# GNN layer on one core: W_uh h made for every node group in the first part, edge sums in four banks of their own

## The chip, the cores and the metric

The kernel runs on one core of one Trainium2 chip. The metric is the time of one execution on the device, in microseconds. A core has TensorE (PE, with its weight loads as PEld), VectorE (DVE), ScalarE (ACT), GpSimd (POOL) and SyncE (SP), which issues the plain DMAs.

## The reference

```python
h = relu(layernorm(x))                                   # 50000 nodes x 128
msg = relu(relu([h[src], h[dst], edge_attr] @ Wm1 + bm1) @ Wm2 + bm2)   # 25000 edges, sorted by dst
agg = segment_sum(msg, dst, 50000)
u = relu([h, agg] @ Wu1 + bu1)                           # = relu(h @ W_uh + agg @ W_ua + bu1)
out = x + h + (u @ Wu2 + bu2)
```

All of it is float32. dst is drawn as 50000 * u**2, so the first nodes receive many edges and the later ones few.

## The kernel before

There are two parts, each with one program per engine.

The first part has 49 steps of 512 edges and 1024 nodes (two groups of 512 nodes). GpSimd gathers the rows of x at both ends of the 512 edges with eight indirect DMAs a step (L278). DVE and ACT normalise edge ends and nodes, TensorE transposes four tiles of 512 columns (L509) and ACT writes them with a relu into `ht` (L457): 0 and 1 are the ends of the edges, 2 and 3 the two node groups. TensorE makes the messages in three pieces (L519 to L521, L529, L535), and ACT moves each from PSUM. Messages stay in SBUF, already multiplied by W_ua. For the even group of a step TensorE also makes W_uh h (L526), which ACT copies over `ht[2]` (L462). The node tiles of both groups (for the odd group still h itself) go to the scratch `ht_scratch`, and x + h to `xh_scratch`.

The second part visits 98 groups of 512 nodes. For each edge tile of 128 edges that can reach the group, DVE makes a one-hot matrix (`hot`, L693), ACT the high part and GpSimd the low part of the messages (`high` L733, `low` L659), and TensorE adds low x hot and high x hot into the group's bank (L784, L785). Which tiles they are is read from a table: at the start of every group each of the four engines loads the group's two numbers into two registers (L626). Every group has at least two tiles, the first group more than twenty. `hot`, `high` and `low` have slots for two groups, and a group may be prepared when the group two before it has been summed (L706, L745). Two banks hold edge sums, two hold outputs.

- For an even group the sum is copied by ACT (`pre_u`, L764), GpSimd adds W_uh h (L680), and ACT makes u (L751). For an odd group TensorE first puts W_uh h into the bank (L810), adds the edge tiles, and ACT makes u straight from the bank.
- The bias of the output is a matmul (`row_sel`, L822) for an even group; for an odd one GpSimd adds it to x + h (L683).
- TensorE multiplies u by W_out (L825), DVE adds x + h (L717), SP stores. SP loads the two scratch tiles of a group ahead, in four slots each.

The engines' programs are unrolled by 4 (TensorE, GpSimd), 8 (DVE) and 2 (ACT, by pairs of groups).

Of the kernel before, what the change touches and what calls it, by code (L numbers as in the profile page):

```python
# [52 lines left out]
def build(nc, x, ends, dst_rows, dst_cols, edge_t, wm1, bm1, wm2, bm2, wu1, bu1, wu2, bu2, out):  # L71
    with ExitStack() as ctx:
# [10 lines left out]
        ht_d = nc.dram_tensor("ht_scratch", (GROUPS, P, W), F32).ap()  # L83
# [15 lines left out]
        ht_i, xh_i = sb("ht_i", [P, 4, W]), sb("xh_i", [P, 4, W])  # L99
# [26 lines left out]
        s_ldh = [sem(f"ht_loaded{i}") for i in range(4)]  # L126
# [7 lines left out]
        s_sum, s_pre_u = sem("edge_sums_copied"), sem("pre_u_ready")  # L134
        s_ut = sem("u_ready")
        s_xb = sem("xh_biased")
# [6 lines left out]
        def load_h(sp, g, slot):  # L143
            sp.dma_start(ht_i[:, slot, :], ht_d[g]).then_inc(s_ldh[slot], 16)
# [5 lines left out]
        with ExitStack() as one:  # L150
# [38 lines left out]
            def sync_1(sp):  # L189
# [40 lines left out]
                def body(s, slot, use):  # L230
                    if not below(s, STEPS - 1) and below(s, STEPS + 1):

                        for g in range(2 * (s - STEPS + 1), 2 * (s - STEPS + 2)):
                            load_h(sp, g, g)
                            load_xh(sp, g, g)
# [4 lines left out]
                    if at_least(s, 3):  # L240
                        to, half = bass.ds(2 * (s - 3), 2), (slot + 1) % 2
                        sp.wait_ge(s_ht, 4 * (s - 2))
                        sp.wait_ge(s_hu, s - 2)
                        sp.dma_start(ht_d[to].rearrange("g p f -> p g f"), ht[:, half, 2:4]).then_inc(s_sto[half], 16)
# [194 lines left out]
            def scalar_1(act):  # L439
                act.wait_ge(s_w, 16 * 11)  # L440

                def body(s, slot, use):
# [45 lines left out]
                    if has_norm:  # L488
# [3 lines left out]
                        relu(range(2, 4))  # L492

                run_steps(act, STEPS + 2, 4, STEPS - 1, 4, body)

            def tensor_1(pe):
# [14 lines left out]

                def messages(s, slot, use, part):
                    if part == 0:
# [9 lines left out]
                        pe.wait_ge(s_ht, 4 * s + 3)  # L523
                        if at_least(s, 1):
                            pe.wait_ge(s_hu, s)
                        pe.matmul(p_hu[:], w_uh[:], ht[:, slot % 2, 2, :], start=True, stop=True).then_inc(s_hus, 1)  # L526
# [30 lines left out]
        with ExitStack() as two:  # L557

            hot = sb("hot", [P, 10, W], F32R, on=two)
            high, low = sb("high", [P, 10, D], F32R, on=two), sb("low", [P, 10, D], F32R, on=two)  # L560
# [5 lines left out]
            out_o = sb("out_o", [P, 4, W], on=two)  # L566
            p_agg, p_out = banks[0:2], banks[2:4]

            def sync_2(sp):
# [28 lines left out]
            class EdgeTiles:  # L598

                def __init__(self, eng, name):
                    self.eng = eng
                    self.regs = [eng.alloc_register(f"{name}_range{i}") for i in range(2)]
# [18 lines left out]
                def visit(self, g, par, regular, more):  # L623

                    eng = self.eng
                    eng.load(self.regs, ranges[0:1, bass.ds(g * 2, 2)])  # L626
                    lo = eng.snap(self.regs[0], min_val=0, max_val=ET - 2)
                    hi = eng.snap(self.regs[1], min_val=2, max_val=ET)
                    regular(lo, 2 * par, 0)
                    with eng.If(hi > lo + 2):  # L630
                        more(lo + 2, 4 + par, None)
                        with eng.If(hi > lo + 3):
                            with eng.Fori(lo + 3, hi, 4) as k:
                                more(k, 6, 0)
                                more(k + 1, 7, 0)
                                with eng.If(hi > k + 2):
                                    more(k + 2, 8, 1)
                                    more(k + 3, 9, 1)
                    regular(lo + 1, 2 * par + 1, 1)

            def gpsimd_2(pool):
# [15 lines left out]
                def low_parts(g, slot):  # L657
# [11 lines left out]
                    tiles.visit(g, slot % 2, regular, more)  # L669

                def body(g, slot, use):
                    if below(g, GROUPS):
                        low_parts(g, slot)
                    if not at_least(g, 1):
                        bias_low()
                    prev = (slot - 1) % 4
# [10 lines left out]
            def vector_2(dve):  # L687
                tiles = EdgeTiles(dve, "dve")

                def onehots(g, slot):  # L690
# [14 lines left out]
                    if at_least(g, 2):  # L705
                        dve.wait_ge(s_agg, g - 1)  # L706
                    tiles.visit(g, slot % 2, regular, more)
# [166 lines left out]
```

## Time and profile before

| | us |
|---|---|
| median of 3 runs | 1107.69 |
| lowest and highest | 1104.02, 1116.73 |
| span of the profiled execution, first to last instruction | 861.7 |
| first part, to the last copy of messages | about 534 |
| second part, first full pair of groups to the end | 565.5 to 861.7 |

The profile gives its own execution by its span alone, and no time of that execution was kept beside it. The median holds 246.0 us more than the span; what lies outside the span is not in any row. One digit of the page's slices is a tenth of a slice of 21.5 us. A busy PE is not PE at its peak: its records overlap.

### The profile page before, as it was taken

Reading aid. Unit: us, or ns where it says so; the run is one execution under the profiler, and the core shown is the slowest. Engines: PE = TensorE matmul, PEld = TensorE weight load, DVE = VectorE, ACT = ScalarE, POOL = GpSimd, SP = SyncE. Lnnn points to the kernel's source line nnn. Section 1 sums busy time; section 2 is a strip of 40 time slices with the busy share of each in tenths; the row PEclk is TensorE's granted clock in tenths of the full one; section 3 lists DMA queues with packets and bytes.
Section 4 is the critical chain, followed back from the end, with each engine's and each line's share of the span. In section 5 each row is a group of like instructions: output and inputs, shape, how many; then the busy total and the mean of one; then the engine's idle time right before and its main releaser. Section 6 shows DMA issues by size and latency. Waiting matters only on the chain. (4 is left out here: it accounts for less than half of the span.)

```text
span 861.7 us, 19736 instructions
## 1 busy us (share of the span) xinstructions
PE 727.2 (84%) x3207; PEld 446.1 (52%) x3208; DVE 666.2 (77%) x2285; ACT 533.4 (62%) x1238; POOL 696.4 (81%) x834
## 2 busy tenths in 40 slices
PE   0688878888898888887787787899999999999998
PEld 0344444444444444443454343566677777676666
DVE  3877787777777777777787775899999988776775
ACT  0666776767676667666687665545555665555554
POOL 7777777777777777777777750899999999898996
PEclk9998998989899999899899999999999999999999
DMA  6466666666666666666676674036688888899897
GB/s 161 125 205 209 219 222 203 215 212 211 203 208 201 204 202 203 206 212 206 209 243 218 196 233 156 0 114 186 191 241 256 273 285 273 275 288 286 285 290 237
DMA packets 99721, 184.50 MB, mean 214 GB/s; under 512 B 15101, under 2 KB 16512, under 8 KB 99700
## 3 DMA queue, kind: packets, MB, share of 16 engines
q1 hardware_dynamic: 87156, 158.57, 56.4%
q0 software_dynamic: 12544, 25.72, 11.0%
q14 instruction: 16, 0.13, 0.1%
q8 instruction: 5, 0.08, 0.0%
HBM read 107.25 MB, written 76.98 MB: 214 GB/s over the span
## 5 line engine op out<-in xcount | busy, mean ns | idle before, releaser
L278 POOL DMA_INDIRECT xg<-x_in,ends_now x392 | 383.3, 978 | 116.2 <-issue 112.9
L693 DVE TENSOR_SCALAR hot<-node,dst_f,minus_base 128x512 fp32r<-128x512 f32 x303 | 212.3, 753 | 42.9 <-issue 30.6
L659 POOL TENSOR_TENSOR low<-msgs,high 128x128 fp32r<-128x128 f32 x303 | 175.4, 603 | 40.7 <-ACT high L733 39.0
L450 ACT ACTIVATE zn<-xn,shift,rstd 128x128 f32<-128x128 f32 x343 | 141.9, 482 | 46.8 <-DVE shift L384 46.1
L784 PE MATMUL bank<-hot,low 128*128 128x512 f32 x303 | 149.1, 492 | 14.3 <-POOL low L659 7.1
L341 DVE BATCH_NORM_STATS2 bn<-xg 128x6 f32<-128x128 f32 x392 | 80.4, 277 | 103.2 <-DMA xg<-x_in,ends_now 103.2
L733 ACT ACTIVATE high<-msgs 128x128 fp32r x303 | 90.1, 310 | 81.3 <-issue 47.2
L785 PE MATMUL bank<-hot,high 128*128 128x512 f32 x303 | 120.4, 397 | 0.0
L509 PE MATMUL bank<-ident,xg 128*128 128x128 f32 x392 | 70.4, 314 | 57.1 <-DVE xg L403 56.7
L526 PE MATMUL bank<-ht,w_uh 128*128 128x512 f32 x98 | 62.8, 727 | 54.0 <-ACT ht L462 54.0
L509 PEld LDWEIGHTS bank<-ident,xg 128*128 128x128 f32 x392 | 49.1, 158 | 112.8 <-issue 87.5
L825 PEld LDWEIGHTS bank<-w_out,u_t 128*128 128x128 f32 x784 | 101.8, 191 | 10.2 <-issue 2.5
L403 DVE TENSOR_SCALAR xg<-xg,mean,rstd 128x128 f32<-128x128 f32 x392 | 106.3, 362 | 0.0
L457 ACT ACTIVATE ht<-bank 128x512 f32<-128x512 f32 x196 | 104.9, 588 | 0.7 <-PE bank L509 0.7
L825 PE MATMUL bank<-w_out,u_t 128*128 128x128 f32 x784 | 103.9, 276 | 0.0
L336 DVE BATCH_NORM_STATS2 bn<-xn 128x6 f32<-128x128 f32 x392 | 98.4, 277 | 0.0
L784 PEld LDWEIGHTS bank<-hot,low 128*128 128x128 f32 x303 | 57.4, 190 | 74.2 <-issue 50.8
L717 DVE TENSOR_TENSOR out_o<-bank,xh_i 128x512 f32<-128x512 f32 x98 | 67.0, 684 | 16.8 <-PE bank L825 15.7
L390 DVE SCALAR_TENSOR_TENSOR xh_o<-zn,xn 128x512 f32<-128x512 f32 x98 | 67.3, 687 | 3.7 <-issue 2.0
L683 POOL TENSOR_TENSOR xh_i<-xh_i,b_out 128x512 f32<-128x512 f32 x49 | 66.7, 1361 | 0.5 <-DMA xh_i<-xh_scratch 0.5
L680 POOL TENSOR_TENSOR pre_u<-pre_u,ht_i 128x512 f32<-128x512 f32 x49 | 64.4, 1314 | 1.4 <-ACT pre_u L764 1.3
L785 PEld LDWEIGHTS bank<-hot,high 128*128 128x128 f32 x303 | 57.9, 191 | 13.1 <-issue 9.2
(85 smaller groups left out, 968.6 us busy)
## 6 DMA issues: line engine op xcount, KB each, us to landing
ht_scratch<-ht SPq DMA_DIRECT2D x49, 512.0 KB
xh_scratch<-xh_o SPq DMA_DIRECT2D x49, 512.0 KB
ht_i<-ht_scratch SPq DMA_DIRECT2D x98, 256.0 KB, 3.7
xh_i<-xh_scratch SPq DMA_DIRECT2D x98, 256.0 KB, 3.5
out<-out_o SPq DMA_DIRECT2D x97, 256.0 KB, 3.6
xn<-x_in SPq DMA_DIRECT2D x48, 512.0 KB
xg<-x_in,ends_now POOLq DMA_INDIRECT x392
edge<-edge_t_in SPq DMA_DIRECT2D x49, 64.0 KB
```

Of the source, the lines that this page charges most:

```text
L278: pool.indirect_dma_start(xg[:, slot, t, :], None, x, bass.IndirectOffsetOnAxis(ap=ends_now[:, slot8, t:t + 1], axis=0)).then_inc(s_xg[slo ...
L336: dve.bn_stats(bn[:, slot % 2, 8 + t, :], xn[:, slot, t, :])
L403: ins = dve.tensor_scalar(to, of, mean[:, slot % 2, t:t + 1], rstd[:, slot % 2, t:t + 1], ALU.subtract, ALU.mult)
L450: ins = act.activation(zn[:, prev % 2, t - 8, :], xn[:, prev, t - 8, :], ACT.Identity, bias=shift[:, prev % 2, t:t + 1], scale=rstd[:, pre ...
L457: act.activation(ht[:, prev % 2, q, :], p_tr[q][:], ACT.Relu).then_inc(s_ht, 1)
L509: ins = pe.transpose(p_tr[q][:, j * P:(j + 1) * P], of, ident[:])
L659: return pool.tensor_tensor(low[:, at, :], msgs[:, k, :], high[:, at, :].bitcast(F32), ALU.subtract)
L693: return dve.tensor_scalar(hot[:, at, :], node[:], dst_f[:, bass.ds(k, 1)], minus_base[:, bass.ds(g, 1)], ALU.subtract, ALU.is_equal)
L733: return act.activation(high[:, at, :], msgs[:, k, :], ACT.Copy)
L784: pe.matmul(to, low[:, at, :], hot[:, at, :], start=start, stop=False, skip_group_check=True)
L785: return pe.matmul(to, high[:, at, :], hot[:, at, :], start=False, stop=stop, skip_group_check=True)
L825: ins = pe.matmul(p_out[half][:, j * D:(j + 1) * D], u_t[:, half, j * P:(j + 1) * P], w_out[:], start=not even, stop=True, skip_group_chec ...
```

## The change

W_uh h is made for both groups of a step in the first part: a second matmul of 512 columns and a second ACT move, now with the bias b_u1 in it (Identity with bias in place of Copy). The scratch holds W_uh h + b_u1 for all groups. In the second part the matmul L810 is gone. An even group goes as before (ACT copy, GpSimd add, ACT relu); for an odd group DVE adds the loaded tile to the bank and ACT makes the relu from SBUF. The output bias is a matmul for every group, and GpSimd's add of it (L683) is gone. Edge sums and outputs have four banks each, `hot`, `high` and `low` have slots for four groups, the registers of four groups are loaded at once (eight numbers), and DVE's last step lies one group later. The output tile lies where `xh_o` was.

```diff
-                    def w_h(s, half):
-                        act.wait_ge(s_hus, s + 1)
-                        act.activation(ht[:, half, 2, :], p_hu[:], ACT.Copy).then_inc(s_hu, 1)
+                    def w_h(s, half, n):
+                        act.wait_ge(s_hus, 2 * s + n + 1)
+                        act.activation(ht[:, half, 2 + n, :], p_hu[:], ACT.Identity, bias=b_u1[:]).then_inc(s_hu, 1)
...
                     if at_least(s, 3):
-                        w_h(s - 3, (slot - 3) % 2)
+                        w_h(s - 3, (slot - 3) % 2, 1)
                     if has_msg:
                         act.wait_ge(s_m1, s - 1)
                         act.activation(m1t[:], p_m1[:], ACT.Relu, bias=b_m1[:]).then_inc(s_m1t, 1)
-                        if not below(s, STEPS + 1):
-                            w_h(s - 2, slot % 2)
+                        w_h(s - 2, slot % 2, 0)
...
+                def w_h(s, slot, n):
+                    pe.wait_ge(s_ht, 4 * s + 3 + n)
+                    if n or at_least(s, 1):
+                        pe.wait_ge(s_hu, 2 * s + n)
+                    pe.matmul(p_hu[:], w_uh[:], ht[:, slot % 2, 2 + n, :], start=True, stop=True).then_inc(s_hus, 1)
...
                     if part == 1:
                         pe.wait_ge(s_m1t, s + 1)
                         pe.matmul(p_m2[:], w_msg[:], m1t[:], start=True, stop=True).then_inc(s_m2, 1)
+                        w_h(s, slot, 1)
...
-            p_agg, p_out = banks[0:2], banks[2:4]
+            out_o = xh_o[:].rearrange("p a b w -> p (a b) w")
+            p_agg, p_out = banks[0:4], banks[4:8]
...
-                        if slot % 2 == 1:
-                            sp.wait_ge(s_pre_u, 2 * use + slot // 2)
-                        else:
-                            sp.wait_ge(s_agg, g - 2)
-                        load_h(sp, g + 1, (slot + 1) % 4)
+                        sp.wait_ge(s_ut, g - 2)
+                        load_hu(sp, g + 1, (slot + 1) % 4)
...
-                def visit(self, g, par, regular, more):
+                def visit(self, g, slot, regular, more):
-                    eng.load(self.regs, ranges[0:1, bass.ds(g * 2, 2)])
+                    if slot == 0:
+                        n = 8 if below(g, GROUPS - 3) else 2 * (GROUPS - g)
+                        eng.load(self.regs[0:n], ranges[0:1, bass.ds(g * 2, n)])
...
-                    if slot % 2 == 1:
-                        pool.wait_ge(s_sum, 2 * use + slot // 2 + 1)
-                        pool.wait_ge(s_ldh[prev], 16 * use + 16)
-                        pool.tensor_tensor(pre_u[:], pre_u[:], ht_i[:, prev, :], ALU.add).then_inc(s_pre_u, 1)
-                    elif at_least(g, 2):
-                        pool.wait_ge(s_ldx[prev], 16 * (use - (slot < 1)) + 16)
-                        pool.tensor_tensor(xh_i[:, prev, :], xh_i[:, prev, :], b_out[:], ALU.add).then_inc(s_xb, 1)
+                    if slot % 2 == 0 and at_least(g, 2):
+                        pool.wait_ge(s_sum, 2 * use + slot // 2)
+                        pool.wait_ge(s_ldh[(slot - 2) % 4], 16 * (use - (slot < 2)) + 16)
+                        pool.tensor_tensor(pre_u[:], pre_u[:], hu_i[:, (slot - 2) % 4, :], ALU.add).then_inc(s_pre_e, 1)
...
+                def add_w_h(g, slot, use):
+                    dve.wait_ge(s_agg, g + 1)
+                    dve.wait_ge(s_ldh[slot], 16 * use + 16)
+                    dve.tensor_tensor(hu_i[:, slot, :], p_agg[slot][:], hu_i[:, slot, :], ALU.add).then_inc(s_pre_o, 1)
...
                 def body(g, slot, use):
                     if below(g, GROUPS):
                         onehots(g, slot)
-                    if at_least(g, 3):
-                        finish(g - 3, (slot - 3) % 4, use - (slot < 3), 2 * use + slot // 2 - 2)
+                    if slot % 2 == 1 and at_least(g, 2) and below(g, GROUPS + 2):
+                        add_w_h(g - 2, (slot - 2) % 4, use - (slot < 2))
+                    if at_least(g, 4):
+                        finish(g - 4, slot, use - 1)
...
+                    if slot % 2 == 1 and at_least(g, 3):
+                        act.wait_ge(s_pre_e, 2 * use + slot // 2)
+                        u_of(g - 3, (slot - 3) % 4, pre_u[:])
+                        act.wait_ge(s_pre_o, 2 * use + slot // 2)
+                        u_of(g - 2, (slot - 2) % 4, hu_i[:, (slot - 2) % 4, :])
...
-                        pe.wait_ge(s_ldh[slot], 16 * use + 16)
-                        if at_least(g, 2):
-                            pe.wait_ge(s_ut, g - 1)
-                        pe.matmul(to, w_uh[:], ht_i[:, slot, :], start=True, stop=False, skip_group_check=True)
+                    if at_least(g, 4):
+                        pe.wait_ge(s_pre_o if slot % 2 else s_sum, 2 * use + slot // 2 - 1)
```

In ACT and DVE the wait ahead of a group's tiles becomes `s_agg >= g - 3` from the fifth group on (before: `s_agg >= g - 1` from the third), and TensorE's program is unrolled by 8, ACT's by 4.

## Rows read from the trace of the kernel before

**Rows 1.** The page: each engine's busy time, share of the span, instructions.

```profile
PE 727.2 (84%) x3207; PEld 446.1 (52%) x3208; DVE 666.2 (77%) x2285; ACT 533.4 (62%) x1238; POOL 696.4 (81%) x834
```

**Rows 2.** Three stretches: length; busy PE, PEld, DVE, ACT, POOL; clock, DMA share, GB/s.

```profile
40.00:500.00 460.00, 379.69 (x1511) 201.13 (x1510) 351.23 (x1687) 316.61 (x713) 354.38 (x378) 0.93 0.64 208
565.50:719.10 153.60, 151.73 (x759) 110.64 (x758) 145.20 (x205) 88.52 (x225) 153.45 (x207) 1.00 0.74 226
719.10:852.40 133.30, 125.96 (x662) 92.81 (x661) 97.45 (x151) 76.89 (x175) 119.01 (x151) 1.00 0.90 286
```

**Rows 3.** Waits in 40 to 500: total us, times, longest.

```profile
POOL xg L278 <- issue: 102.8, 347, 0.3
DVE bn L341 <- DMA xg<-x_in,ends_now: 97.1, 33, 4.8
PE bank L526 <- ACT ht L462: 50.7, 27, 3.4
PE bank L509 <- DVE xg L403: 25.6, 47, 1.2
...
POOL xg L278 <- PE bank L509: 3.0, 10, 0.3
```

**Rows 4.** Groups in 40 to 500: count, busy us, mean ns, idle before.

```profile
L278 POOL DMA_INDIRECT xg<-x_in,ends_now  x357 | 348.1, 975 | 105.9 <-issue 102.8 <-PE bank L509 3.0
L526 PE MATMUL bank<-ht,w_uh 128*128 128x512 f32 x90 | 58.3, 735 | 50.7 <-ACT ht L462 50.7
L462 ACT ACTIVATE ht<-bank 128x512 f32<-128x512 f32 x45 | 26.5, 589 | 0.0
```

**Rows 5.** Groups in 565.5 to 719.1 (23 pairs of groups).

```profile
L693 DVE TENSOR_SCALAR hot<-node,dst_f,minus_base 128x512 fp32r<-128x512 f32 x159 | 119.8, 808 | 7.9 <-issue 6.6 <-PE bank L785 0.7
L659 POOL TENSOR_TENSOR low<-msgs,high 128x128 fp32r<-128x128 f32 x160 | 94.6, 618 | 0.1
L683 POOL TENSOR_TENSOR xh_i<-xh_i,b_out 128x512 f32<-128x512 f32 x24 | 32.9, 1369 | 0.0
L717 DVE TENSOR_TENSOR out_o<-bank,xh_i 128x512 f32<-128x512 f32 x46 | 31.3, 680 | 0.5
```

**Rows 6.** Timeline of GpSimd, one pair of groups with six tiles: start, us.

```profile
641.99 1.84 POOL L659 TENSOR_TENSOR low<-msgs,high 128x128 fp32r<-128x128 f32 x3
...
648.08 1.83 POOL L659 TENSOR_TENSOR low<-msgs,high 128x128 fp32r<-128x128 f32 x3
```

**Rows 7.** Timeline of DVE, a late group.

```profile
800.31 1.18 DVE L693 TENSOR_SCALAR hot<-node,dst_f,minus_base 128x512 fp32r<-128x512 f32 x2 [0.66 <-issue]
```

**Rows 8.** The chain of waits within one pair of 12 tiles: start, us, what.

```profile
565.69 0.23 PE bank L822
565.92 0.89 PE bank L825 x8
566.81 0.86 PE bank L810 x2
567.67 0.23 PE bank L784
...
570.96 1.00 POOLq L626
```

**Rows 9.** Register loads in 533 to 561 and from 600: ns, least/median/most.

```profile
L626 POOLq TENSOR_LOAD <-ranges x3: 518/528/888, 534.7 to 558.3; - x3
...
L626 DVEq TENSOR_LOAD <-ranges x86: 523/600/1460, 604.4 to 851.1; - x86
```

**Rows 10.** Groups in 719.1 to 852.4 (24 pairs of groups).

```profile
L693 DVE TENSOR_SCALAR hot<-node,dst_f,minus_base 128x512 fp32r<-128x512 f32 x103 | 67.2, 695 | 22.3 <-issue 15.1 <-PE bank L785 7.1
```

**Rows 11.** Two stretches with much DMA, columns as in Rows 2.

```profile
765.00:770.00 5.00, 4.42 (x22) 2.66 (x20) 3.23 (x6) 2.69 (x6) 4.51 (x6) 1.00 0.99 350
...
820.00:840.00 20.00, 18.74 (x100) 13.46 (x99) 15.62 (x23) 11.08 (x25) 17.95 (x25) 1.00 0.92 294
```

**Rows 12.** DMA issues: KB each, median us to landing; 98 loads of xh_i likewise.

```profile
ht_i<-ht_scratch SPq DMA_DIRECT2D x98, 256.0 KB, 3.7
```

More of the change, by code:

```diff
@@ L124, in build @@
         s_sto = [sem(f"scratch_stored{i}") for i in range(2)]
-        s_ldh = [sem(f"ht_loaded{i}") for i in range(4)]
+        s_ldh = [sem(f"hu_loaded{i}") for i in range(4)]
         s_ldx = [sem(f"xh_loaded{i}") for i in range(4)]
@@ L140, in build, with load_hu @@
         s_out = [sem(f"out_stored{i}") for i in range(4)]
[L143 to L144 removed]
+        def load_hu(sp, g, slot):
+            sp.dma_start(hu_i[:, slot, :], hu_d[g]).then_inc(s_ldh[slot], 16)
         def load_xh(sp, g, slot):
@@ L492, in body @@
                         relu(range(2, 4))
+                    if not below(s, STEPS + 1):
+                        w_h(s - 2, slot % 2, 1)
                 run_steps(act, STEPS + 2, 4, STEPS - 1, 4, body)
@@ L521, in messages @@
                         pe.matmul(p_m1[:], w_edge[:], edge[:, slot, :], start=False, stop=True).then_inc(s_m1, 1)
[L523 to L526, printed above, removed]
+                        w_h(s, slot, 0)
                     if part == 1:
@@ L557, in build @@
         with ExitStack() as two:
-            hot = sb("hot", [P, 10, W], F32R, on=two)
-            high, low = sb("high", [P, 10, D], F32R, on=two), sb("low", [P, 10, D], F32R, on=two)
+            hot = sb("hot", [P, 16, W], F32R, on=two)
+            high, low = sb("high", [P, 16, D], F32R, on=two), sb("low", [P, 16, D], F32R, on=two)
             pre_u = sb("pre_u", [P, W], on=two)
@@ L603, in __init__ @@
                     self.eng = eng
-                    self.regs = [eng.alloc_register(f"{name}_range{i}") for i in range(2)]
+                    self.regs = [eng.alloc_register(f"{name}_range{i}") for i in range(8)]
                     self.count = eng.alloc_register(f"{name}_count")
@@ L703, in more, with finish @@
                         onehot(k, at).then_inc(s_hot_x, 1)
-                    if at_least(g, 2):
-                        dve.wait_ge(s_agg, g - 1)
-                    tiles.visit(g, slot % 2, regular, more)
-                def finish(g, slot, use, odd_before):
+                    if at_least(g, 4):
+                        dve.wait_ge(s_agg, g - 3)
+                    tiles.visit(g, slot, regular, more)
+                def add_w_h(g, slot, use):
+                    dve.wait_ge(s_agg, g + 1)
+                    dve.wait_ge(s_ldh[slot], 16 * use + 16)
+                    dve.tensor_tensor(hu_i[:, slot, :], p_agg[slot][:], hu_i[:, slot, :], ALU.add).then_inc(s_pre_o, 1)
+                def finish(g, slot, use):
                     dve.wait_ge(s_o, g + 1)
-                    if slot % 2 == 1:
-                        dve.wait_ge(s_xb, odd_before + 1)
-                    else:
-                        dve.wait_ge(s_ldx[slot], 16 * use + 16)
+                    dve.wait_ge(s_ldx[slot], 16 * use + 16)
                     if at_least(g, 4):
                         dve.wait_ge(s_out[slot], 16 * use)
-                    dve.tensor_tensor(out_o[:, slot, :], p_out[slot % 2][:], xh_i[:, slot, :], ALU.add
-                                      ).then_inc(s_fin, 1)
+                    elif not at_least(g, 1):
+                        for half in range(2):
+                            dve.wait_ge(s_sto[half], 32 * ((STEPS + 1 - half) // 2))
+                    dve.tensor_tensor(out_o[:, slot, :], p_out[slot][:], xh_i[:, slot, :], ALU.add).then_inc(s_fin, 1)
                 def body(g, slot, use):
@@ L742, in more, with u_of @@
                         part(k, at).then_inc(s_hi_x, 1)
-                    if at_least(g, 2):
-                        act.wait_ge(s_agg, g - 1)
-                    tiles.visit(g, slot % 2, regular, more)
-                def u_of(g, half, of):
+                    if at_least(g, 4):
+                        act.wait_ge(s_agg, g - 3)
+                    tiles.visit(g, slot, regular, more)
+                def u_of(g, slot, of):
                     if at_least(g, 2):
                         act.wait_ge(s_o, g - 1)
-                    act.activation(u_t[:, half, :], of, ACT.Relu, bias=b_u1[:]).then_inc(s_ut, 1)
+                    act.activation(u_t[:, slot % 2, :], of, ACT.Relu).then_inc(s_ut, 1)
                 def body(g, slot, use):
@@ L779, in sums @@
                 def sums(g, slot, use):
-                    to = p_agg[slot % 2][:]
-                    even = slot % 2 == 0
+                    to = p_agg[slot][:]
                     def add(at, stop, start=False):
@@ L790, in regular @@
                         pe.wait_ge(s_lo, 2 * g + n + 1)
-                        ins = add(at, n == 1, n == 0 and even)
+                        ins = add(at, n == 1, n == 0)
                         if n == 1:
```

92 lines of the change are left out of this document (38 added, 54 removed).

## The prediction

> **What bounds the kernel now.** I read the page first for its totals [rows 1], then split the span by stages, because a mean over two parts with different limits hides both [rows 2]. The first part advances by one step of eight gathers each 460 / (357 / 8) = 10.31 us. Its bound is in the groups [rows 4]: a gather takes 975 ns and leaves 296 ns of issue time behind it (105.9 / 357), 1.27 us together, and eight are 10.2 us. GpSimd waits for another engine for 3.0 us in all of this stretch, while DVE waits 97.1 us for gathered rows [rows 3]. TensorE is busy 379.7 of 460 us, 8.51 us a step, and idle 1.80 us a step. So the first part goes at the pace at which GpSimd issues gathers, with TensorE second.
>
> In the second part I take a pair of groups as the unit, since the two kinds of groups alternate. From 565.5 to 719.1 there are 23 pairs of 6.68 us with 159 tiles (6.9 a pair), and GpSimd is busy 153.45 of 153.6 us with DVE behind it at 145.2 [rows 2]. The timeline shows what that full GpSimd does in a pair of six tiles: 6.09 us from 641.99 to 648.08, of which six low parts at 0.60 us (three in 1.84, overlapping a little) are 3.6 us and the two long adds (L680, L683) 1.25 us each [rows 6]. From 719.1 to 852.4 there are 24 pairs of 5.55 us with 4.3 tiles each. No engine is full there (TensorE 126.0, GpSimd 119.0, DVE 97.5 of 133.3 us), DMA has a share of 0.90 at 286 GB/s, and DVE waits 15.1 us before its one-hots for nothing but its own sequencer [rows 2, 10]. That is the register load: 523 to 1460 ns each group [rows 9], and in the chain it stands between two pieces of work, 1.00 us of it at 570.96 [rows 8].
>
> **First part, step by step.** Each of the 49 steps gets one more 512-column matmul on TensorE and one more 589 ns move on ACT [rows 4]. The present matmul costs 58.3 us over 45 steps, 1.30 us; at full clock two such passes take 0.86 us start to start, as L810 shows [rows 8]. That makes TensorE 8.51 + 1.30 = 9.81 us of 10.31 a step. I cost it at nothing on the path: its cover is the idle 1.80 us, of which 50.7 us (1.13 a step) lie before L526, where TensorE waits for ACT, and 25.6 us (0.57) before the transposes L509, where it waits for DVE [rows 3]. The new matmul stands just before those transposes and eats that wait first. If the cover were gone the whole 1.30 us would show, less the 0.50 left: see the rivals. TensorE's new wait (for the first move by ACT, before the second matmul) has the transposes and message matmuls queued behind it; but the message matmul L529, of the same size, stands in front, and ACT's move takes 0.59 us. ACT is busy 316.6 of 460 us, so 26.5 us more fits. The store of the scratch waits for the same move of ACT as before, and its bytes and number are unchanged. When the gathers are over this part drains, and there the last move of ACT comes after the last copy of messages: +0.6 us on the path, with a semaphore 0.7. **First part: +0.7 us**, bounds 0 and +1.5 apart from the rival.
>
> In the stretch of the first part the granted clock is 0.93, a mix of 2.4 GHz and 1.2 GHz; in the second part, where TensorE is hardly ever idle, it is 1.00 throughout [rows 2]. In "TensorE: Matmul & The Clock Gate", Part 1, the Trainium skill says that TensorE falls to half rate after idling. By that rule the extra matmul would raise the clock of the first part; the sum takes no credit for it.
>
> **Second part, early pairs.** Taken off GpSimd: L683, 1369 ns, once a pair [rows 5]. GpSimd's load falls from 6.67 us a pair by 1.25 start to start, to about 5.4. Taken off TensorE: L810, 0.86 us a pair; added there: one L822, 0.23 [rows 8]. So neither sets the pace any more, and what is late next is DVE. Its load is 145.2 / 23 = 6.31 us a pair. The change adds one PSUM add of the shape of L717, 680 ns [rows 5]. It also relieves DVE: a one-hot takes 808 ns on average here [rows 5], against 0.59 us in a late group (two in 1.18) [rows 7]. The excess, 0.218 x 159 = 34.7 us, I put to waiting beside the 47 long adds of GpSimd (24 of L683 and 23 of L680) (0.74 us each), as the one-hots that run beside those are the long ones; the low parts cost only hundreds of nanoseconds. One of two long adds goes: -0.74 a pair if that is so, nothing if the one-hots are slowed by GpSimd's work in general. DVE's load becomes 6.31 + 0.68 - 0.74 = 6.25, or 6.99 without relief. To 6.25 I add 0.1 for what remains of its idle time (8.4 us in 23 pairs now, most of it before register loads). That is 6.35 against 6.68: **-0.33 a pair, -7.6 us in 23 pairs**; bounds -0.74 x 23 = -17 (all of DVE's idle time gone and more) and (6.99 - 6.68) x 23 = +7.
>
> Waits that change: a group is prepared when the group four before it is summed, not two. The chain now passes from the sums of one group through the preparation of the next [rows 8]; with four slots this loop opens, and TensorE follows the producers. DVE's new add waits for the sums of the group two before, and behind it are queued the output add and the next one-hots; TensorE has two groups of time for these, so I cost it at nothing. ACT's relu of the odd group now waits for DVE's add, with the next high parts behind it and GpSimd's low parts behind those; GpSimd has 1.2 us a pair to spare for that. SP's order stays load, load, store, each behind waits of about the same age.
>
> **Late pairs.** By the same steps a pair needs on DVE 97.45 / 24 + 0.69 less half of 0.105 x 103 / 24, that is 4.5 us; on GpSimd 119.0 / 24 - 1.37 = 3.6; on TensorE 4.3 tiles x 0.46 + 2 x 0.89 + 2 x 0.23 = 4.2 [rows 2, 5, 8, 10]. The transfers are what is left: a pair moves six tiles of 256 KB [rows 12], 1.573 MB, and now takes 5.55 us for them. The fastest 20 us that I found run at 294 GB/s with a share of 0.92, a stretch of 5 us at 350 with 0.99 [rows 11]. Those would be 5.35 and 4.5 us a pair. I take 5.2 us (302 GB/s), nearer to the long stretch, since a rate must be held for 130 us: **-0.35 a pair, -8.4 us in 24 pairs**; bounds -0.2 and -0.95 a pair (DVE's 4.5 plus 0.1). The stretch ahead of 565.5, with the first two groups, I cost at nothing: more than half of its tiles belong to one group and go through the slots that are as few as before. The drain at the end gains an add by DVE of 0.7 us, and loses a register load of as much.
>
> **The register load.** Four loads of two registers become one of eight. The trace has no load of eight. From below it costs as much as one of two (0.52 us), from above four times that, 2.1 us, in one piece. I take about 1 us, near the end below: at 534.7 all four engines load together, eight registers in all, and the slowest took 888 ns [rows 9]. Then it is nearly covered by the operation queued on the engine.
>
> "Runtime: NRT & Kernel Launch", in the section on instruction fetch, the Trainium skill gives about 200 ns for each register, even in bulk. By that figure eight would be an estimated 1.6 us, which speaks for the upper end and for the second rival.
>
> **Sum.** 0.7 - 7.6 - 8.4 = -15.3 us. The profiled execution goes from a span of 861.7 to 846.4; with the 246.0 us that the median holds outside the span, 1107.7 becomes **1092 us** (1088 to 1099).
>
> **Rivals.**
> - *The transfers don't bind late* (350 GB/s can be held): late pairs go at 4.6 us, 24 x 0.95 = -22.8, with the early gain and the first part -29.7, 1078 us. For it: single stretches of 5 us at that rate. Against: never for 20 us.
> - *The load grows with its registers*: 2.1 us in one piece, of which 0.6 is covered by one queued operation, so 1.5 us a four-group round, 0.75 a pair, on DVE. Early pairs become 6.25 + 0.75 = 7.0, +7.4 us in all; late ones 4.5 + 0.75 = 5.25, -7.2. With +0.7 that is 1109 us. Loads of up to 1460 ns speak for it.
> - *DVE takes GpSimd's place without relief*: early +7, late -8.4, first part +0.7: 1107 us.
> - *TensorE becomes the bound of the first part* (slower): the waits for DVE and ACT are tied to the step and aren't eaten. Then a step is 8.51 + 1.30 + 1.80 = 11.6 us in place of 10.31, +1.3 x 48 = +62, less 16: 1154 us. It decides as soon as load and waits exceed 10.31, that is when less than 1.30 of the 1.80 us of idle time can be used; if 0.5 us of step time showed it would be 1116. Against it: the new matmul stands where TensorE waits, and GpSimd waited for TensorE hardly at all, so that a late step can be caught up.
>
> **Chances.** The forecast 0.45, transfers not binding 0.13, load by registers 0.20, no relief 0.12, TensorE in the first part 0.10. A difference of 1% (11 us) is about what a measurement of this kernel can tell from none. Faster by more (under 1096.6): most of the first and all of the second, 0.56; slower by more (over 1118.8): 0.08; the rest 0.36. The range leaves out half of the fast rival and the slow one: 1078 to 1112.
>
> **What the profile after should show.** Steps of the first part still of 10.3 us, L526 twice as often, and the idle time before it smaller. GpSimd no longer full in early pairs and DVE at 97% or more; one-hots shorter than 808 ns. A pair of six tiles in about 5.75 us. Late, DMA at or over 300 GB/s with a share above 0.95 and register loads only each fourth group. I am wrong if the step of the first part grows beyond 10.5 us, if the loads take 2 us and stand in the chain, or if a late pair stays at 5.5 us with DMA still at 286 GB/s: then latency along the chain of a group, not transfers, set its pace.

## The result, and the profile after

The kernel after takes 1114.1 us (median of 20 runs, 1108.7 to 1120.6), the kernel before 1109.5 (20 runs, 1098.5 to 1116.7): ratio 1.007, 95% interval 1.0045 to 1.0096. The forecast was 1092, a gain of 15.3 us; what came is a loss of 4.6. Medians here are of all runs of a kernel, while ratios leave out slow runs (over 1.5% above the fastest of their kernel), so in a few places the two don't divide out exactly.

The profiled execution of after took 1113.5 us with a span of 1110.7: only 2.8 us lie outside its span. So the 246 us that the median of before holds above its span of 861.7 can't be time outside the span. The traced execution of before can't have been like the timed ones. Its chip is not known, but the experiments met both cases: on three chips the first part of every run went without stalls (e1 to e6, e15 to e18), on two it stalled in every kernel that gathers without a pause (e7 to e14). Each chip was used at one time only, so whether it is the chip or its condition at that time is not known; below I say chips with and without stalls. The first part of after ends at 804.5 us (before: 534.4), the second takes 306.2 us (before: 327.3). First the three stretches that answer to [rows 2]: length, busy time of PE, PEld, DVE, ACT, POOL, then clock, DMA share, GB/s.

```profile
70.00:690.00 620.00, 406.56 (x1420) 203.99 (x1419) 314.43 (x1493) 310.26 (x670) 302.76 (x331) 0.78 0.43 136
837.50:983.20 145.70, 132.27 (x736) 107.28 (x734) 144.69 (x231) 77.12 (x226) 120.31 (x184) 1.00 0.78 240
983.20:1101.10 117.90, 106.30 (x638) 88.41 (x636) 113.58 (x173) 64.67 (x175) 87.91 (x128) 1.00 0.97 319
```

In the first line every engine is idle for a third of the time or more, GpSimd for half, and the clock is 0.78. In the second, DVE has taken GpSimd's place (99% busy against 83%). In the third DMA is at a share of 0.97. The waits of the first part of after, answering to [rows 3]:

```profile
POOL ends_now L258 <- PE bank L492: 232.5, 20, 14.8
DVE r L351 <- ACT sd L448: 196.6, 33, 13.7
ACT msgs L467 <- remote: 127.9, 18, 11.4
```

GpSimd, which waited 3.0 us for the transposes in before, now waits 232.5 us for them, 11.6 us in each of 20 waits. One round of the timeline of after (start, us, idle time before and what ended it; "remote" is a semaphore whose sender the profile doesn't name):

```profile
394.18 0.19 POOL L258 COPY ends_now<-ends_all 128x16 int32 x1 [12.24 <-PE bank L492]
...
401.97 1.06 PE L522 MATMUL bank<-w_ua,m2t 128*128 128x128 f32 x8
...
403.25 0.58 ACT L439 ACTIVATE ht<-bank 128x512 f32<-128x512 f32 x1
...
405.54 0.18 DVE L343 SCALAR_TENSOR_TENSOR var<-pair,sq 128x16 f32<-128x16 f32 x1 [1.70 <-remote]
...
406.93 0.60 ACT L439 ACTIVATE ht<-bank 128x512 f32<-128x512 f32 x1 [3.09 <-remote]
...
413.70 0.95 POOL L260 DMA_INDIRECT xg<-x_in,ends_now  x1 [0.30 <-issue]
417.60 0.60 ACT L467 ACTIVATE msgs<-bank 128x512 f32 x1 [10.07 <-remote]
...
425.94 0.21 POOL L258 COPY ends_now<-ends_all 128x16 int32 x1 [11.30 <-PE bank L492]
```

GpSimd issues gathers from 394.9 to 414.7 without a pause. For the first 9 us the others work at their usual pace. Then handovers come late: DVE waits 1.7 us at 405.54 for a semaphore that its own instruction before last was to raise, and ACT stands idle for 10 us until 417.60, though the matmuls that it waits for (L522) ended at 403.0. In most rounds of this trace that copy starts 2.7 to 3.0 us after the last gather has been issued. Only then does the work go on, at its usual pace again, and GpSimd stands still until the transposes of 425.6. A round of two steps takes 31.9 us on average, where two steps took 20.7 in the trace of before.

The second part, one-hots and low parts of the 23 early pairs of after, to be read against [rows 5], and its register loads against [rows 9]:

```profile
L672 DVE TENSOR_SCALAR hot<-node,dst_f,minus_base 128x512 fp32r<-128x512 f32 x161 | 107.1, 720 | 0.7 <-PE bank L771 0.3 <-issue 0.3
L645 POOL TENSOR_TENSOR low<-msgs,high 128x128 fp32r<-128x128 f32 x160 | 88.4, 579 | 25.4 <-ACT high L720 25.4
```

```profile
L612 DVEq TENSOR_LOAD <-ranges x23: 352/1148/1591, 857.6 to 1095.9; - x23
L612 POOLq TENSOR_LOAD <-ranges x23: 548/597/1430, 857.6 to 1095.2; - x23
```

### The profile page after: what moved, and what is told of

Same layout as the page of the kernel before. It is cut to its first block and busy times, and to the rows that moved or that the text cites. A ratio compares the mean times of both kernels' runs of the same rounds, so it can differ in the third digit from the quotient of the medians.

```text
span 1110.7 us, 19375 instructions
## 1 busy us (share of the span) xinstructions
PE 779.5 (70%) x3256; PEld 472.2 (43%) x3257; DVE 686.8 (62%) x2334; ACT 547.6 (49%) x1287; POOL 620.9 (56%) x785
## 5 line engine op out<-in xcount | busy, mean ns | idle before, releaser
L499 PE MATMUL bank<-ht,w_uh 128*128 128x512 f32 x196 | 132.4, 763 | 111.1 <-ACT ht L444 108.6
L351 DVE RECIPROCAL r<-sd 128x16 f32<-128x16 f32 x49 | 12.4, 253 | 253.2 <-ACT sd L448 238.9
L508 PE MATMUL bank<-ht,w_src 128*128 128x512 f32 x98 | 69.3, 796 | 137.0 <-issue 75.5
L770 PE MATMUL bank<-hot,low 128*128 128x512 f32 x303 | 132.0, 435 | 5.0 <-POOL low L645 4.7
L499 PEld LDWEIGHTS bank<-ht,w_uh 128*128 128x128 f32 x196 | 37.5, 227 | 200.4 <-ACT ht L439 126.2
L385 DVE TENSOR_SCALAR xg<-xg,mean,rstd 128x128 f32<-128x128 f32 x392 | 105.7, 355 | 2.0 <-issue 2.0
L467 ACT ACTIVATE msgs<-bank 128x512 f32 (+1 forms) x49 | 29.2, 596 | 143.4 <-remote 139.0
L720 ACT ACTIVATE high<-msgs 128x128 fp32r x303 | 80.6, 304 | 38.5 <-PE bank L771 18.9
L444 ACT ACTIVATE ht<-bank,b_u 128x512 f32<-128x512 f32 x98 | 68.1, 695 | 46.3 <-PE bank L499 37.4
L492 PE MATMUL bank<-ident,xg 128*128 128x128 f32 x392 | 54.7, 284 | 40.8 <-DVE xg L385 32.1
L508 PEld LDWEIGHTS bank<-ht,w_src 128*128 128x128 f32 x98 | 17.9, 229 | 145.8 <-issue 85.4
```

The lines of the kernel that those rows point to most:

```text
L385: ins = dve.tensor_scalar(to, of, mean[:, slot % 2, t:t + 1], rstd[:, slot % 2, t:t + 1], ALU.subtract, ALU.mult)
L499: pe.matmul(p_hu[:], w_uh[:], ht[:, slot % 2, 2 + n, :], start=True, stop=True).then_inc(s_hus, 1)
L720: return act.activation(high[:, at, :], msgs[:, k, :], ACT.Copy)
L770: pe.matmul(to, low[:, at, :], hot[:, at, :], start=start, stop=False, skip_group_check=True)
```

## The experiments

Every ratio is to runs of before on the same chip. **Chips without stalls** (before 861): one for e1 to e3, one for e4 to e6, one for e15 to e18. **Chips with stalls** (before 1130 and 1111): one for e7 to e10, one for e11 to e14.

**e1, before unchanged.**

> The kernel before, unchanged, profiled again. Theory A (the timed runs of both kernels stall in the first part, and the profiled execution of before was one without the stalls): span near 1105 us, a first part of some 775 us in place of 534 with stalls of GpSimd of about 11 us in every second step, and a second part of 327 us as in the trace of before. Theory B (before has no stalls, and 246 us lie outside its span while only 3 us lie outside that of after): span near 862 us again, time near 1109.

862.5 us, span 860.7, first part 533.0 us, no stall; before beside it 861.4. Theory B's span of 862 came, but not its time of 1109: here only 1.7 us lie outside the span, so the 246 us are no fixed cost. It needed a trace of before on a chip with stalls (e11).

**e2, only the first part's share.** To the kernel before:

```diff
-                        act.activation(ht[:, half, 2, :], p_hu[:], ACT.Copy).then_inc(s_hu, 1)
+                        act.activation(ht[:, half, 2 + n, :], p_hu[:], ACT.Copy).then_inc(s_hu, 1)
...
                         pe.matmul(p_m2[:], w_msg[:], m1t[:], start=True, stop=True).then_inc(s_m2, 1)
+                        w_h(s, slot, 1)
```

> The kernel before with only the first part's share of the change: the second W_uh matmul and ACT move of each step; the second part is unchanged and applies W_uh once more to the odd groups, so their output is not that of the reference. Theory A (the stall ends at a fixed point of a chain through TensorE and ACT, so added work there is paid in every round of two steps): 49 matmuls of 0.86 to 1.3 us, 20 to 35 us slower than before, 1130 to 1145. Theory B (hidden beside the gathers, my prediction): within 2 us of before.

865.6 us, ratio 1.0033 (1.0009 to 1.0057). Without stalls the extra work is hidden: the last step of gathers starts at 501.7 us against 501.5 in e1. The 4 us come behind the gathers: the last copy of messages ends at 535.4 against 533.0, the first one-hot starts at 539.6 against 534.4.

**e3, only the second part's share.** To the kernel after, the matmul and move are as before:

```diff
-                        w_h(s, slot, 1)
...
-                        act.activation(ht[:, half, 2 + n, :], p_hu[:], ACT.Identity, bias=b_u1[:]).then_inc(s_hu, 1)
+                        act.activation(ht[:, half, 2, :], p_hu[:], ACT.Copy).then_inc(s_hu, 1)
```

> The kernel after without the second W_uh matmul and ACT move in the first part: the odd groups add h in place of W_uh h, and the bias b_u1 is left out, so the output is not that of the reference. Theory A: the second part's gain alone, 20 us (306 against 327 us), so 1085 to 1092. Theory B (the second part gives nothing, and something else in the first part moved): 1105 to 1115. If the stalls of the first part react to the extra work, the difference to the kernel after is 20 to 30 us.

842.1 us, ratio 0.979 (0.9756 to 0.9826): the gain of the second part alone.

**e4, after unchanged.**

> The kernel after, unchanged. Theory A (the time depends on whether this chip lets the first part stall; the second part gains 20 us on any chip, and the first part loses 3 to 4 us without stalls, some 25 us with them): where the kernel before takes about 861 us, the kernel after takes 845 (ratio 0.981); where before takes about 1109, it takes 1114. Theory B (the whole difference of 1.007 is in the kernels, not in the stalls): ratio 1.00 to 1.01 on any chip.

847.0 us, ratio 0.982 (0.9788 to 0.9855). The same kernel that lost 0.7% gains 1.8% here. The ratios of e2 and e3 multiplied are 0.982 as well. e15, on a third such chip, gave 0.980.

**e5, register loads for each group.** To the kernel after:

```diff
-                    if slot == 0:
-                        n = 8 if below(g, GROUPS - 3) else 2 * (GROUPS - g)
-                        eng.load(self.regs[0:n], ranges[0:1, bass.ds(g * 2, n)])
+                    eng.load(self.regs[2 * slot:2 * slot + 2], ranges[0:1, bass.ds(g * 2, 2)])
```

> The kernel after with the register loads of before: two registers, once a group, into each group's own pair of registers. Theory A (a load of eight costs nearly the same as one of two, so one load in four groups saves idle time of DVE, which sets the pace): 5 to 12 us slower than the kernel after, as each group's load leaves 0.2 to 0.6 us of idle time on DVE. Theory B (a load of eight takes four times as long and stands in the path): same or faster than the kernel after.

848.4 us beside 847.0, ratios 0.9844 (0.9814 to 0.9875) and 0.9822. The two can't be told apart by time; the profiled spans differ by 3.5 us. Theory A's 5 to 12 us did not come, and nothing speaks for Theory B: the load is worth a few us at most.

**e6, GpSimd's second long add put back.** To the kernel after:

```diff
+                    if slot % 2 == 1 and at_least(g, 2):
+                        if at_least(g, 4):
+                            pool.wait_ge(s_twice, 2 * use + slot // 2 - 1)
+                        pool.tensor_tensor(b_out[:], node[:], b_out[:], ALU.add).then_inc(s_twice, 1)
```

> The kernel after with GpSimd's second long add a pair put back: it adds node and b_out in SBUF for each odd group, 128 x 512, and nobody waits for it. Theory A (DVE's one-hots are held up beside each long add by 0.74 us): 47 x 0.3 to 0.74 us, 14 to 35 us slower than the kernel after, and the mean one-hot of the early pairs back near 800 ns. Theory B (the long adds don't hold DVE up; GpSimd has the time to spare): within 3 us of the kernel after.

865.0 us, 18 us more than e4, ratio 1.004 (1.0019 to 1.0058): the gain of the second part is gone. Nobody waits for this add. The one-hots of the early pairs of e4, then of e6:

```profile
L672 DVE TENSOR_SCALAR hot<-node,dst_f,minus_base 128x512 fp32r<-128x512 f32 x161 | 108.0, 726 | 1.0 <-issue 0.6 <-PE bank L771 0.3
```

```profile
L677 DVE TENSOR_SCALAR hot<-node,dst_f,minus_base 128x512 fp32r<-128x512 f32 x161 | 120.6, 804 | 0.6 <-issue 0.6
```

At 804 ns they are back at the 808 of before [rows 5]. An early pair takes 6.89 us against 6.40, a late one 5.21 against 4.93. DVE is busy 157.9 of 158.5 us in e6's early pairs, so the longer one-hots go straight into the time; GpSimd is not full (151.9). The trace shows where they are longer: of the 160 one-hots there, the 60 that run beside a long add for more than 0.2 us average 1044 ns, the other 100 average 653. In the trace of before it is 1058 ns for 55 and 667 for 103.

**e7, the second matmul behind the first transposes.** To the kernel after:

```diff
-                        w_h(s, slot, 1)
                     if part == 2:
+                        w_h(s, slot, 1)
```

> The kernel after with the second W_uh matmul of a step moved from in front of the first two transposes to behind them. Where the first part has no stalls both orders are hidden beside the gathers: Theory A 842 to 848 us, as the kernel after (847) within 3 us. Theory B (the place of the matmul costs even beside running gathers): 3 us or more faster than the kernel after. Where it has stalls: Theory A 20 to 25 us faster than the kernel after (1090), since the matmul no longer stands between DVE's normalised ends and the transposes for which GpSimd waits; Theory B no different from it.

This chip stalls: 1135.1 us, before 1129.7, ratio 1.0014 (0.9975 to 1.0053). Theory A's 20 us did not come. The kernel after did not run on this chip, so whether the moved matmul is a few us better stays open (after's ratios on two other chips are 1.007 and 1.010).

**e8 to e10, stop and go by a tighter wait.** In before, after and moved:

```diff
-                        pool.wait_ge(s_tr, 4 * (s - 2) - 2)
+                        pool.wait_ge(s_tr, 4 * s - 2)
```

> The kernel before with GpSimd's wait tightened, so that a pair of gather steps starts only when the first two transposes of the step just gathered are made. It copies, on a chip without stalls, the stop and go that the trace of the kernel after shows: two steps of gathers, 20.4 us, then a wait of some 10 to 12 us. Both theories: 1080 to 1160 us. It is the base for the next two.

> The kernel after with the same tightened wait. Theory A (in each wait the second W_uh matmul stands in front of the transposes, 0.9 to 1.1 us on the path in each of 24 waits): first part 21 to 27 us longer than in the locked kernel before, second part 16 to 20 us shorter, so 0 to +10 us, ratio to it 1.000 to 1.009, as the 1.007 of the result. Theory B (the extra work is hidden in stop and go too): 13 to 19 us faster than the locked kernel before.

> The kernel with the moved matmul and the same tightened wait. Theory A: 18 to 25 us faster than the locked kernel after, 13 us or more faster than the locked kernel before. Theory B (it is ACT's extra move, not the place of the matmul, that costs): within 5 us of the locked kernel after.

They came to the chip with stalls, not to one without, so the wait came on top of the late handovers: 1213.3, 1232.3 and 1233.0 us, ratios 1.074 (1.070 to 1.078), 1.090 (1.084 to 1.096) and 1.092 (1.088 to 1.096). The split, from the traces (first part; then means over 21 rounds: GpSimd's wait, of it up to ACT's last square root, and from there to GpSimd's restart):

| | first part | wait | to the root | from it |
|---|---|---|---|---|
| e8, before | 889.4 | 16.21 | 10.03 | 6.19 |
| e9, after | 924.9 | 17.55 | 10.39 | 7.16 |
| e10, moved | 920.1 | 17.49 | 11.33 | 6.16 |

e9 is 19 us slower than e8, where its Theory A said 0 to 10: its first part is 35.5 us longer, more than the 21 to 27 forecast. The moved matmul leaves the stretch after the root (7.16 back to 6.16) and comes back in the one before it (10.39 to 11.33), where it stands ahead of the last transposes and so of the root. Theory A of e10 has fallen: with this tighter wait both places are on the path. Theory B's number came true (e10 within 1 us of e9), but its reason, ACT's extra move, is not shown: nothing was run with the move alone.

**e11 to e13, the parts on one chip with stalls.**

> The kernel before once more, for a trace of it on a chip on which its first part stalls, should this be one. Theory A: there the trace shows rounds of two gather steps (20.4 us) and a wait of GpSimd for the transposes of 9 to 12 us, a first part of 775 to 800 us and a second part of 322 to 328. On a chip without stalls: 861 us, nothing new.

> The kernel after. On a chip with stalls, Theory A (the added matmul, move and handovers of a step lengthen each of 24 waits of GpSimd by 1 us or more): first part 20 to 35 us longer than before, second part 16 to 20 shorter, ratio 1.002 to 1.012. Theory B (the first part is as long as that of before, and the 1.007 came from elsewhere): ratio 0.982 to 0.99. On a chip without stalls: 0.982.

> The kernel before with only the first part's share of the change (the odd groups get W_uh twice, so the output is not that of the reference). On a chip with stalls, Theory A: 20 to 35 us slower than before, ratio 1.018 to 1.032, the whole of it in the first part. Theory B: within 5 us of before. On a chip without stalls: ratio 1.003, as in its earlier run.

Before: 1110.7 us (13 runs); e11 is the one profiled execution, 1101.5 us. After: 1119.4, ratio 1.010 (1.005 to 1.015). First part only: 1135.3, ratio 1.022 (1.013 to 1.031). In the traces the first part takes 773.5 us in before, 807.4 in after, 804.4 in e13; the second 326.2, 308.2 and 325.0. A round is 30.87, 32.36 and 32.01 us, over 22 waits in each trace. So the share of the first part alone costs 24.6 us by the medians, 30.9 in these traces, all of it in the first part. This is the wait's end in e11, from the moment when messages move again to GpSimd's restart:

```profile
307.35 0.60 ACT L486 ACTIVATE msgs<-bank 128x512 f32 x1 [10.73 <-remote]
...
308.80 0.23 ACT L466 ACTIVATE sd<-veps 128x16 f32<-128x16 f32 x1
...
309.66 2.05 PE L526 MATMUL bank<-ht,w_uh 128*128 128x512 f32 x2 [8.46 <-ACT ht L462]
...
311.21 2.13 DVE L403 TENSOR_SCALAR xg<-xg,mean,rstd 128x128 f32<-128x128 f32 x8
...
311.50 1.92 PE L529 MATMUL bank<-m1t,w_msg 128*128 128x512 f32 x2
...
313.21 1.12 PE L509 MATMUL bank<-ident,xg 128*128 128x128 f32 x8
...
314.74 0.20 POOL L276 COPY ends_now<-ends_all 128x16 int32 x1 [10.09 <-PE bank L509]
```

and in e12:

```profile
318.55 0.60 ACT L467 ACTIVATE msgs<-bank 128x512 f32 x1 [9.40 <-remote]
...
320.00 0.23 ACT L448 ACTIVATE sd<-veps 128x16 f32<-128x16 f32 x1
...
320.95 2.05 PE L499 MATMUL bank<-ht,w_uh 128*128 128x512 f32 x2 [6.64 <-ACT ht L444]
...
322.41 2.13 DVE L385 TENSOR_SCALAR xg<-xg,mean,rstd 128x128 f32<-128x128 f32 x8
...
322.79 1.91 PE L515 MATMUL bank<-m1t,w_msg 128*128 128x512 f32 x2
...
324.49 1.91 PE L499 MATMUL bank<-ht,w_uh 128*128 128x512 f32 x2
...
326.20 1.43 PE L492 MATMUL bank<-ident,xg 128*128 128x128 f32 x8
...
328.03 0.20 POOL L258 COPY ends_now<-ends_all 128x16 int32 x1 [12.28 <-PE bank L492]
```

From the messages' move to the restart it is 7.4 us in e11 and 9.5 in e12. DVE starts on the rows (L403, L385) 3.86 us after the messages' move in both; the second L499, 1.71 us start to start, stands between L515 and the transposes (L492), and TensorE works without a gap from the first L499 on. In this round two passes cost twice the 0.86 of [rows 8]: the granted clock is 0.50 (1.2 GHz) from 320.9 to 326.2, after TensorE has stood idle for 6.64 us. Over the 21 long waits of e12 it is 0.86 to 1.71 us from the second L499 to the transposes, 1.17 on average. On average GpSimd's wait is 10.81 us in e11 and 12.25 in e12, of the difference 1.31 after the root. So the second matmul would be most of it; ACT's move was not separated from it.

**e14, a pause after every step of gathers.** To the kernel after:

```diff
...
+                    pool.wait_ge(s_xg[slot], 128 * (2 * use8 + slot8 // 4) + 128)
+                    pool.tensor_tensor(tick[:], msgs[:, ET, 0:8], msgs[:, ET, 8:16], ALU.add).then_inc(s_tick, 1)
```

> The kernel after, in which GpSimd waits after every step of eight gathers until they have landed, and then does a small add. Theory A (handovers of the other engines are late only when GpSimd has issued gathers for some 9 us without a pause): on a chip with stalls a step takes 12 to 14 us and is never followed by a long wait, so the first part takes 600 to 700 us in place of 800, the kernel 900 to 1000. Theory B (the delay comes with gathers as such, however they are grouped): the delays stay, and the kernel is as slow as the kernel after or slower. On a chip without stalls the pause costs 2 to 5 us a step: 940 to 1090 us.

971.5 us on the chip with stalls, ratio 0.875 (0.871 to 0.880). The first part takes 660.8 us in place of 807.4, a step 12.9 on average. In its trace the wait for the landing stands before the small add, and the longest wait of ACT for messages falls from 10.7 us in e12 to 3.7:

```profile
312.10 0.94 POOL L262 DMA_INDIRECT xg<-x_in,ends_now  x1 [0.30 <-issue]
314.66 0.20 POOL L270 TENSOR_TENSOR tick<-msgs 128x8 f32<-128x8 f32 x1 [1.62 <-DMA xg<-x_in,ends_now]
```

```profile
ACT msgs L475 <- remote: 60.4, 31, 3.7
```

The delay itself is still there: ACT's copy starts 1.3 to 1.9 us after the last gather of a step has been issued. It ends sooner because the gathers do. With the same pause on a chip without stalls (e17) not one such wait is in the trace. Theory A held in its sizes; that it is the wait for the landing that helps, and not the small add or the lower rate of gathers, was not separated.

**e15 to e18, one chip without stalls.**

> The kernel after, as the base for the next three on one chip. With stalls: ratio 1.002 to 1.012; without: 0.982.

> The kernel after with the second W_uh matmul behind the first two transposes, beside the kernel after on the same chip. With stalls, Theory A (this matmul is the last thing but one that GpSimd's wait waits for): 8 to 22 us faster than the kernel after, and on average a wait 0.4 to 0.9 us shorter. Theory B (any added handover costs wherever it stands): within 5 us of it. Without stalls: within 3 us of it.

> The pause after every step of gathers together with the moved matmul. With stalls: as the drained kernel after (971) or up to 10 us faster. Without stalls: the pause costs 2 to 5 us a step, 940 to 1090 us, so that it is no gain there.

> The kernel before with the pause after every step of gathers. Theory A (the change loses on chips with stalls only by what it adds to GpSimd's long waits, so with the waits gone it gains its second part's 18 us again): 10 to 20 us slower than the drained kernel after (971), 980 to 990. Theory B (the added work of the first part costs on such a chip with or without the waits): equal to it or faster.

After 845.4 (0.980, 0.976 to 0.984), moved 847.5 (0.983, 0.980 to 0.987): the place of the matmul makes no difference that can be measured. With the pause, moved takes 970.5 (1.126, 1.123 to 1.130) and before 987.7 (1.147, 1.143 to 1.151): the change gains 17 us there too. e18's theories were about a chip with stalls, and it didn't meet one, so they stay untested. The pause gives nearly the same time on both kinds of chip (971.5 in e14; 970.5 in e17, which differs from it by the place of the matmul), 12% under before on the one and 13% over it on the other. No version that was run beats both kernels on both kinds.

## Why the prediction was wrong, step by step

**The step that failed is the first part's +0.7 us ("I cost it at nothing on the path"), read from the wrong execution.** The prediction put the 246.0 us between median and span outside the span and left them unchanged. They were the stalls of the first part in the timed runs, 773.5 against 534 us (e11). With that, the profile that I read was not like the executions that were timed, and the cover that it showed, GpSimd's unbroken gathers, was not there in them. Where the first part stalls its share of the change costs 24.6 us (e13, by medians) in place of 0.7, and that is more than the second part gains. A span that falls 22% short of the median of the same kernel was the sign, and the prediction named it and went on.

**The first part in detail.** Nothing on the path is right where nothing stalls: e2 and e4 have gather steps of 10.3 and 10.4 us still, and TensorE's idle time took up the matmul (busy 410.81 of 460 us in e4 against 379.69 in [rows 2], at a clock of 0.96; 403.47 at 0.98 in e2):

```profile
40.00:500.00 460.00, 410.81 (x1618) 212.77 (x1618) 353.15 (x1701) 349.87 (x765) 354.81 (x376) 0.96 0.65 209
```

It is wrong where the first part stalls: there the cover is gone in each of 22 long waits, and the added matmuls and moves make a round 1.49 us longer (e12 against e11), 34 us in all in those two traces. The rival for TensorE had the right place (waits for DVE and ACT that can't be used) and the wrong reason: TensorE was not the bound of a step, it was busy 401 of 620 us in e12. I had given a case like it 1116 us; that 1114 came is chance, since that case knew nothing of stalls.

By the Trainium skill, "TensorE: Matmul & The Clock Gate", Part 1, TensorE falls to half rate after idling. The traces agree: the granted clock is 0.78 in the stalled part, with TensorE idle for a third of it, against 0.93 and 0.95 (before, e1) without stalls, and in some waits that made the added matmul twice as dear. That more work raises the clock without stalls is less clear: 0.96 in e4 and 0.98 in e2, against those 0.93 and 0.95.

**The change of parts** was put at 0.7 us. The first one-hot comes 3.7 us later in e4 than in the trace of before (539.5 against 535.8). ACT's last move ends 0.6 us after its last copy of messages, and only behind it does SP issue the last two stores to the scratch: the second of them at 536.2 us in e4, against 532.1 before, where they left ahead of that copy. I had counted the move alone.

**Early pairs** were to go from 6.68 to 6.35 us: 6.33 in after, 6.40 in e4. The reason holds too: DVE is the bound at 99%, and e6 shows the relief by putting the add back. Its size was not the 0.74 us for each add that I took: e6 gives 0.49 us an early pair and 0.28 a late one. I had put all of a one-hot's excess over 590 ns to the long adds, but one-hots that don't run beside one average 667 ns in before too; that leaves (1058 - 667) x 55 / 46, or 0.47 us for each of its 46 long adds.

**Late pairs** were put at 5.20, with DMA as the bound at 302 GB/s. They take 4.91 us in after, at 319 GB/s and a share of 0.97 for 118 us. DMA is nearly full as forecast, but DVE at 96% is as near, and no run shows which of the two sets the pace. DVE's load came out at 4.7 us a pair, not 4.5: late one-hots got longer (769 ns on average against 695 before [rows 10]), not shorter. The rate was mis-sized by 6%: the 20 us of the old trace at 294 GB/s were no limit, since 319 was held here. Against the forecast of -0.35 a pair that is -0.6, some 7 us more in 24 pairs; it makes up for the 3 us that the change of parts cost beyond its 0.7 and for what the early pairs fell short.

**The register load** of eight takes 597 ns on GpSimd and 1148 on DVE (medians), against 600 for two on DVE [rows 9] and 790 on GpSimd: the "about 1 us" was right, and the rival by registers (2.1 us) is out. The 200 ns for each register of the Trainium skill, "Runtime: NRT & Kernel Launch", section on instruction fetch, would be an estimated 1.6 us for eight; here both medians disagree, and only DVE's longest load, 1591 ns, comes near it.

**Together:** without stalls 861.7 to 844.0 us (e4), where 846.4 was forecast, and ratios of 0.982 and 0.980. That it lies so near is in part luck, since the late pairs' error and the others cancel. With stalls the second part gains 18 us (326.2 to 308.2) and the first loses 34 in the profiled executions; by the medians of that chip the loss is 9 us net, by the 20 runs of the result 5.

**Open:** why handovers come late on some chips when gathers run for more than 9 us. The runs show when it sets in, when it ends and that a pause helps, not its cause. Whether a shorter pause would do was not tried, nor what the matmul and the move cost in a stall one by one, nor whether the late pairs are bound by DMA or by DVE.

## What to carry to other kernels

Set the span of the profile against the times before anything else: when they differ by much more than a few us, the trace may show an execution unlike those timed, and a cover read from it may not exist. Work that is hidden behind one engine's steady stream shows in the stops of that stream; moving it elsewhere in the loop that ends the stop need not help (e9 and e10 took the same time). GpSimd operations on SBUF that nobody waits for can still cost DVE time.

## What the runs showed of the hardware

- On the two chips of e7 to e14 and in the result's trace, semaphores between and within engines come late from about 9 us after the start of uninterrupted indirect DMAs by GpSimd: ACT's copy of messages starts some 14 us after the matmuls that it waits for have ended, and 2.5 to 3.1 us after the last gather has been issued, in most rounds of after, e11 and e12. On the three other chips kernels with the same gathers show no such wait. With a wait for each step's landing the kernel after took 971.5 us in place of 1119.4.
- A 128 x 512 add by GpSimd in SBUF, waited for by nobody, makes the kernel 18 us slower over 47 of them: 0.38 us each, with DVE's one-hots at 804 in place of 726 ns in the early pairs (1044 beside a long add, 653 elsewhere, e6).
- Transfers of 2 KB rows, two loads and one store for each group, ran at 319 GB/s for 118 us at a share of 0.97.
- A register load of eight numbers took no longer than one of two on GpSimd (median 597 ns in after, 790 for two in before), and about twice as long on DVE (1148 against 600 ns).
